# Entangling-layer cross terms and controls on the vector engine, and new piece orders, in a two-layer transformer kernel

## The reference, cut to what matters

```python
s1 = state[:, :, :-1]
s2 = state[:, :, 1:]
ctrl = jnp.abs(s1) ** 2
rot = cos_t * s2 + sin_t * jnp.exp(1j * phi) * jnp.conj(s2)
new = ctrl * rot + (1.0 - ctrl) * s2
state = jnp.concatenate([new, state[:, :, -1:]], axis=2)
```

## Time and profile before

| | us |
|---|---|
| median of 3 runs | 2605.27 |
| lowest, highest | 2596.32, 2612.04 |
| profiled execution: its own time | 2586.84 |
| profiled execution: its span | 2585.0 |
| PE, DVE, ACT, POOL busy | 1995.3, 1998.8, 1283.5, 1428.3 |

### The profile page before, as it was taken

How to read it: one execution, slowest core, us unless ns; L and a number is a source line. 1 busy time by engine, 2 the same in 40 slices (tenths; PEclk the granted TensorE clock), 3 DMA queues, 4 the chain that set the end, 5 groups by cost and what they waited for, 6 DMA issues and landing times.

```text
span 2585.0 us, 45044 instructions
## 1 busy us (share of the span) xinstructions
PE 1995.3 (77%) x15068; PEld 1548.3 (60%) x15068; DVE 1998.8 (77%) x3422; ACT 1283.5 (50%) x2989; POOL 1428.3 (55%) x1104
## 2 busy tenths in 40 slices
PE   1357877888877888787788788888788787289999
PEld 0346666666666666666666666666666664157777
DVE  4888999989989998999999999899999852502221
ACT  1125555555555555555555555555555555033332
POOL 2666666666666665666666666666666510364310
PEclk8688899889899988989988988888988887589999
DMA  3000000000000000000000000000000000112210
GB/s 89 2 7 9 9 8 8 8 8 8 8 8 8 9 9 6 8 9 9 8 8 8 8 8 8 8 8 8 8 8 6 6 5 5 34 44 63 56 45 24
DMA packets 64565, 39.38 MB, mean 15 GB/s; under 512 B 9350, under 2 KB 60431, under 8 KB 64528
## 3 DMA queue, kind: packets, MB, share of 16 engines
q1 hardware_dynamic: 54238, 26.30, 3.6%
q0 software_dynamic: 4096, 8.40, 1.2%
q10 hardware_dynamic: 6194, 4.21, 0.6%
HBM read 26.31 MB, written 12.58 MB: 15 GB/s over the span
## 4 chain that ended last, share of the span: by engine, by line
POOL 32%; PE 25%; issue 19%; DVE 17%; ACT 5%; ACTq 1%; POOLq 0%; DVEq 0%; DMA 0%
POOL arena L649 10%; POOL arena L657 8%; PE pa L1296 4%; PE pd L1286 4%; DVE arena L629 4%; PE pb L1036 4%; POOL arena L461 4%; POOL arena L662 3%; POOL arena L629 3%; POOL arena L458 2%; PE pa L732 2%; DVE arena L525 2%; PE pd L1027 2%; DVE state L529 2%; PE pd L1024 2%
## 5 line engine op out<-in xcount | busy, mean ns | idle before, releaser
L751 PE MATMUL pa<-ident,arena 128*128 128x128 f32 x4096 | 545.9, 291 | 99.9 <-POOL arena L629 66.4
L751 PEld LDWEIGHTS pa<-ident,arena 128*128 128x128 f32 x4096 | 514.8, 205 | 122.7 <-POOL arena L629 79.9
L649 POOL TENSOR_TENSOR arena<-arena,neg_half 128x32 f32<-128x32 f32 x64 | 269.4, 4226 | 281.9 <-DVE arena L495 281.9
L1036 PE MATMUL pb<-ident,arena 128*128 128x128 f32 x1536 | 304.7, 313 | 138.2 <-ACT arena L931 84.2
L657 POOL TENSOR_TENSOR arena<-state,c_cross 128x448 f32<-128x448 f32 x128 | 241.6, 1908 | 226.6 <-DVE state L518 188.2
L1036 PEld LDWEIGHTS pb<-ident,arena 128*128 128x128 f32 x1536 | 194.6, 158 | 271.4 <-issue 172.9
L931 ACT ACTIVATE arena<-pb 128x384 f32<-128x384 f32 x512 | 253.9, 496 | 155.9 <-PE pb L1036 151.3
L629 DVE TENSOR_TENSOR arena<-arena 128x1024 f32<-128x1024 f32 x192 | 311.8, 1638 | 4.1 <-PE pa L751 3.3
L924 ACT ACTIVATE arena<-pd,arena 128x256 f32<-128x256 f32 x512 | 245.7, 480 | 0.0
L458 POOL TENSOR_TENSOR arena<-arena,eps_t 128x2 f32<-128x2 f32 x128 | 126.8, 991 | 213.4 <-DVE arena L490 125.8
L923 ACT ACTIVATE arena<-pd,arena 128x128 f32<-128x128 f32 x512 | 189.6, 370 | 37.7 <-DVE arena L811 36.6
(11 more groups left out here) (246 smaller groups left out, 4577.0 us busy)
## 6 DMA issues: line engine op xcount, KB each, us to landing
x_land<-in_L_attn_query SPq DMA_DIRECT2D x32, 128.0 KB, 2.1
arena<-in_L_attn_query SPq DMA_DIRECT2D x32, 128.0 KB, 2.1
x_scratch<-x SPq DMA_DIRECT2D x32, 128.0 KB, 1.8
xn_scratch<-xn_d SPq DMA_DIRECT2D x32, 128.0 KB, 1.8
arena<-x_scratch SPq DMA_DIRECT2D x16, 256.0 KB, 3.0
out_x<-arena SPq DMA_DIRECT2D x16, 256.0 KB, 2.4
w<-in_L_ffn_W ACTq DMA_DIRECT2D x1, 2048.0 KB
arena<-xn_scratch,arena POOLq DMA_INDIRECT x128, 2.5
```

Of the source, the lines that this page charges most:

```text
L649: g.tensor_tensor(of_tile(rnorm)[:, :, c], of_tile(ssq)[:, :, c], of_tile(neg_half)[:, :, c], ALU.pow).then_inc(S("a_rnorm"), 1)
L751: mm = pe.matmul(pa[:, t, c * P:c * P + P], wprod[:, k % NWP, j * 128:j * 128 + 128], ident[:, :], start=(j == 0), stop=(j == NH - 1))
L1036: mm = pe.transpose(pb[:, j * P:j * P + P], p_raw[:, s % 3, j * P:j * P + P], ident[:, :])
```

## The change

The cross terms and the control of layers 2 and 3 move from `gpsimd_a` to `vector_a`; the waits for POOL go, and the control's wait for ACT's squares (`a_m`) goes along to DVE. POOL's stage A has 3 pieces in place of 7, DVE's has 23 in place of 17. The instructions themselves are the same in shape. The semaphores `a_cross` and `a_ctrl` are no longer used.

```diff
-DVE_A_STEPS = 15
+DVE_A_STEPS = 21
...
-POOL_ORDER = "A1C2B1A3C1A1B1A2C1D1C1D1"
-ACT_ORDER = "E7A1E3A1E4B1E2A1E5B1E1C1E1B1E2C1E3A1E2B1E3C1E4A1E3C1A1D1B1D1C1D2"
-PE_ORDER = "E5A1E3A1E4B1E3B1E7B1E2B1E3C1E1C1E1C1E1C1D1C1D1C1D1C2D2C2"
-DVE_ORDER = "C1A1C1A1C1B1C1E1C1E1B1C1E1C2E1C1A1C1A1C1E1C4B1C1B1E1C2A1E1B1C1B1C1A1E1A1B1C1A1C2B1A1B1C1A2C1A1D2C1A1C1D3C1A2C2D2A1D1A1D1C1"
+POOL_ORDER = "A1C2B1A1C2B1C1D1A1D1"
+ACT_ORDER = "E7A1E5A1E2B1E2A1E4B1E3C1B1E2C1E6A1B1C1E3A1E6D1C1A1D1C1D1B1D1"
+PE_ORDER = "E4A1E4A1E4B1E3B1E7B1E2B1E2C1E1C1E1C1E1C1E1C1D1C1D2C3D2C1"
+DVE_ORDER = "C1A1C1A1C1B1C1E1B1E1C2E1C2E1C2E1C2A1C2A1C2B1C1E1C2B1C1E1A1B1A1B1A1C1B1C2A1E1B2A2C1A1C1A3C1A1D2A2D1A1C1D2C1A3C2D2A1D1A1D1C1"
...
                 v.wait_ge(S("a_state"), 3 * b + 1 + l)
                 yield from L(v.tensor_tensor(gate_p[:, :, :, :], st[:, :, :, HD:E],
                                   c_diag[:, l, :, 0:GW].unsqueeze(2).broadcast_to([P, 2, 4, GW]), ALU.mult))
-                v.wait_ge(S("a_cross"), 2 * b + l)
+                for c in range(2):
+                    yield from L(v.tensor_tensor(gate_r[:, c, :, :], st[:, 1 - c, :, HD:E],
+                                                 c_cross[:, l, 0:GW].unsqueeze(1).broadcast_to([P, 4, GW]), ALU.mult))
                 yield from L(v.tensor_tensor(g8(gate_p), g8(gate_p), g8(gate_r), ALU.add))
-                v.wait_ge(S("a_ctrl"), 2 * b + l)
+                v.wait_ge(S("a_m"), 3 * b + 1 + l)
+                yield from L(v.tensor_tensor(gate_m[:, :, :], gate_sq[:, 0, :, :], gate_sq[:, 1, :, :], ALU.add))
...
-            st = state[:, :, :, :, :].rearrange("p c t k n -> p c (t k) n")
-            for l in range(1, DEPTH):
-                g.wait_ge(S("a_state"), 3 * b + 1 + l)
-                for c in range(2):
-                    ins = g.tensor_tensor(gate_r[:, c, :, :], st[:, 1 - c, :, HD:E],
-                                          c_cross[:, l, 0:GW].unsqueeze(1).broadcast_to([P, 4, GW]), ALU.mult)
-                ins.then_inc(S("a_cross"), 1)
-                yield
-                g.wait_ge(S("a_m"), 3 * b + 1 + l)
-                g.tensor_tensor(gate_m[:, :, :], gate_sq[:, 0, :, :], gate_sq[:, 1, :, :], ALU.add).then_inc(S("a_ctrl"), 1)
                 yield
```

## The result

| | before | after |
|---|---|---|
| median (lowest to highest), us | 2606.97 (2596.32 to 2612.04) | 2501.47 (2499.69 to 2502.82) |
| runs | 4 | 4 |
| profiled execution, us | 2586.84 | 2502.82 |
| its span, us | 2585.0 | 2501.0 |

Two kernels of the experiments have executions of two lengths, with different granted clocks; a ratio given for one of them compares only the shorter ones.

What follows compares the result with a forecast made beforehand. DVE was taken as the bound, a round being its work plus waits. Rounds falling from 64.33 to 62.4 us save 56 us over 29, filling and draining rounds 8: 2605 - 64, about 2541 us; range 2475 to 2600.

Steps and rivals of the forecast that it cites:

- Added to DVE, +3.2 us: Per round, four cross terms and two controls of 448 elements on DVE, 0.53 us each: +3.2 us.
- DVE busy in the full rounds: From 1693 us, falls slightly or stays: +93 for the added work, -60 to -170 for collisions.
- Collisions after, 1 to 4.7 us: Per-round DVE time lost to meeting POOL instructions: 6.9 us before, 1 to 4.7 after, a gain of 2.2 to 5.9.
- one of each: Of POOL products W3 and W7, one well and one badly placed against DVE: rounds of 61.9 to 62.4 us; chance 0.45.
- A's double good placement: Rival: both POOL products miss DVE's two-input pieces, 112 us saved, 2493 us; chance 0.22.
- B's double bad one: Rival: both POOL collisions fall badly, rounds of 63.6 to 64.3 us, 2580 to 2605 us, nothing measurable; chance 0.2.
- L821 48.3 to 52.0 us into the round: Start of DVE's L821 in a round, by placement of W3 and W7; 48.56 us in the trace before.
- Tail 11.6 us: Chain from the start of L821 to L612, the round's end: 11.6 us, where the trace has 15.8.
- L637's second wait to 1.3: DVE's wait at the second L637 falls from 2.3 us by round to about 1.3.
- The half projection beside DVE's last pieces: At the round's end, DVE's last pieces run beside L759's second half alone on PE: 2.0 us in place of 3.4.
- rival C: Slower: L821 late, the chain behind it does not shrink; rounds of 65.3 us, 2634 us; chance 0.13.
- 62.4 us taken: Length of a full round after the change, from 64.33 us; taken nearer the bad end, saving 56 us over 29 rounds.

Runs made afterwards that it cites:

- e_dummy_tt: Changed kernel plus six 448-element products and sums on POOL, from constants into tiles nobody reads; 2664.83 us, ratio 1.0280 to the kernel before.
- e_w7_dve: Changed kernel with product 7 on DVE, behind L812, in place of POOL; 2680.10 us, ratio 0.9626 to before, from its shorter executions.
- e_dummy_pow: Changed kernel plus four small powers on POOL (14 and 7 elements per partition) that read next to nothing; 2597.83 us, ratio 1.0027 to before.
- e_y_back: Changed kernel with both halves of the C projection after the logits again on PE; 2600.56 us, ratio 0.9626 to before.
- e_alloc: Changed kernel's split of work with the kernel before's piece orders on all engines; 2608.06 us, ratio 1.0062 to before.
- w_before: Kernel before plus 75 unread identity matmuls by round on PE, PE's first piece of A one piece earlier; 2700.57 us, ratio 1.0401 to before.
- w_after: Changed kernel plus 44 unread identity matmuls by round where PE stands idle; 2506.48 us, ratio 0.9662 to before.
- e_d_first: Changed kernel with L811 and L812 ahead of L532 on DVE; 2659.19 us, no ratio given; before took 2701.97 there.
- w2_d_first: Changed kernel with L811 and L812 ahead of L532, plus idle-time identity matmuls on PE; 2493.31 us, ratio 0.9562 to before.

## Why the prediction was right, and where it was off

- **What bounds the kernel**: right. DVE is at 95% in the full rounds now (1689.0 of 1785.1 us), and the time followed its work and its waits.
- **Added to DVE, +3.2 us**: right. Controls 626 ns, expected 614; cross terms 765 in the mean, of which 0.15 (0.6 us by round) is the collision with POOL's bias L669, which I had not listed.
- **DVE busy in the full rounds**: 1692.9 to 1689.0. That is +93 for the added work and so about -97 for collisions, 3.3 us by round; forecast were 2.2 to 5.9.
- **Collisions after, 1 to 4.7 us**: by the excess of the profile about 3.1, with W3 well placed (0.2) and W7 in L532 (1.8; priced 2.05). This is the case of one of each that I took. My condition, that DVE's next instruction reads two tiles, was too narrow: the clip L637 reads one, and takes up to 1358 ns before (429 at the median) and 693 in the mean in e_dummy_tt, against 422 in after. e_dummy_tt and e_w7_dve show the mechanism by adding it and taking it away. The Trainium skill's lock (page "SBUF — State Buffer", section "SBUF: two separate sides") fits again: the loser's excess, 2.90 - 1.09 = 1.8 us, is about what was left of POOL's product when it came, 1033.47 - 1031.52 = 1.95.
- **Rivals A and B**: A's double good placement and B's double bad one did not come; one product fell each way. The time lies nearest to A's number all the same, for reasons outside A's mechanism (below), so the range held in part by luck: its low end was A's.
- **L821 48.3 to 52.0 us into the round**: 50.1. **Tail 11.6 us**: 11.35. Both right; norm D starts at once, as said. e_dummy_pow shows that this start is worth 1.7 us by round and more: (67.9 - 16.1) / 30 in the wait alone.
- **L637's second wait to 1.3**: it went to 0.5. L612's to nothing: right. **L505**: no wait came.
- **The half projection beside DVE's last pieces**: the step was written as 2.0 us in place of 3.4, as part of the tail. e_y_back undoes it at no cost: 3.4 would have been hidden as well. The step was not needed, though the tail's total was right.
- **A new wait from the new orders (rival C)**: none. But e_alloc shows a form of C that is real: with the old orders L821 waits 2.0 us for PE and the move gains nothing. I had priced C from DVE's side only, and had not seen how much PE's 16 matmuls between turn and projection weigh once DVE comes sooner; I had booked them as 0.35 us.

**The mis-sized term** is the round: 62.4 us taken, 61.56 measured. For the case that came, W3 well and W7 badly placed, my parts give 47.9 + 0.4 + 2.05 + 11.6 = 61.95; I took 62.4, the figure of the opposite case and the upper end of "61.9 to 62.4". The other 0.4 is the net of smaller things: L812 comes at 50.1 and not 50.35 (W7's price), the tail takes 11.35 and not 11.6, which gives the 61.4 of nearly every round, and the first full round, 65.3 us, lifts the mean by 0.13. That is 29 x 0.84 = 24 us; the filling rounds brought 6.8, the draining ones nothing and the experts' part -3.2, where I had 8. So the profiled saving is 84 us and not 64.

**The level** is the other 21 us. I carried the saving over to the runs as a constant. But the runs of before lie 10 to 25 us above its profiled execution, those of after within some 3 us of theirs. Before's rounds differ among themselves (62.7 to 67.0 us), those of after are nearly all 61.4. The third slice of a round has a low clock in both kernels, 0.50 to 0.63 in every full round of before. What sets before's long rounds apart is their end: four of the 29 take 66.6 to 67.0 us, about 2.9 more than the others' mean, or 12 of the 80.4 us gained in the full rounds. The slice from 60 to 65 us of a 67.0 and of a 64.3 us round of before:

```profile
1020.70:1025.70 5.00, 3.76 (x17) 3.07 (x17) 2.75 (x7) 2.38 (x6) 0.81 (x2) 0.50 0.09 26
...
1215.30:1220.30 5.00, 4.17 (x22) 3.77 (x22) 3.53 (x10) 1.38 (x4) 0.22 (x1) 0.66 0.09 26
```

The clock was nowhere in the sum. More such rounds in the other executions of before would explain the 21 us. That is argued, not shown: these executions have no trace, and w_before does not tell it. Of the 13 executions of before on the chip of e_alloc the four shortest (2581.88 to 2587.81) have a mean clock of 0.882 to 0.886 and the four longest (2593.09 to 2597.27) 0.876 to 0.878; among the 11 on the chip of w_after the link is weak.

## What to carry to other kernels

When work moves from a contended helper engine to the bound one, price three things: the work, the collisions it ends, and the queue it leaves on the helper, ahead of a short piece of the critical chain. Don't move work without moving the orders of the other engines: here neither half alone gained. With the old orders a sum on PE stood between two links of the chain and held DVE; with the old split POOL's cross terms stood ahead of norm D and met DVE's instructions. And look at the granted clock in slices of a round before you compare rounds; one kernel's rounds can differ by 9% with it (60.3 to 66.0 us in e_d_first). A pattern that repeats makes the time steady, not short: it is 61.4 us by round in after and 64.85 in e_w7_dve. Filling PE's idle time raised the clock here and did not shorten the rounds of after.

## What was unexpected in the hardware

- One program gives rounds of 60.3 to 66.0 us in one execution, by the place where the granted clock falls (e_d_first). Elsewhere one pattern repeats itself in nearly every round (after, e_alloc, e_w7_dve). With some 20 small matmuls by round e_d_first's longer ones were gone (w2_d_first), but so were its rounds of 60.3. In after, neither 19 nor 44 of them made the steady rounds shorter than 61.4, though the clock was 0.94 to 1.00 in their mean and not 0.92.
- Chips differ by about 100 us: before takes 2701.97 us on one, and 2590 to 2609 in the other four sets of runs. On the slow one all four traces, all of variants of after, have it at one place: the part behind the last L615, the experts', takes 573 to 581 us, and 475 in after. From e_y_back's waits (after has 221.4 us for the first and nothing like the second; the profile doesn't name the second's releaser):

```profile
DVE arena L1226 <- PE pa L1287: 248.4, 30, 78.9
DVE arena L1226 <- remote: 71.2, 2, 35.6
```

- A power on few elements is dear on POOL. From the groups of POOL in e_dummy_pow:

```profile
L661 POOL TENSOR_TENSOR dummy_x<-eps_t,neg_half 128x14 f32<-128x14 f32 x64 | 194.0, 3031 | 7.9 <-DVE state L520 4.1 <-DVE state L534 3.7
```

14 elements per partition take 3.0 us, more than a product of 1024.
